# Layer 0 attention: the causal mask is added by VectorE on the way out of PSUM, not accumulated by TensorE

## The reference

```python
def _L0_attn_ref(x, Wq, Wk, Wv, Wo):            # x is the adapter's output for the item
    q, k, v = heads(x @ Wq.T), heads(x @ Wk.T), heads(x @ Wv.T)      # 32 heads of 16
    q = q * cos + rotate_half(q) * sin
    k = k * cos + rotate_half(k) * sin
    scores = jnp.einsum('bhqd,bhkd->bhqk', q, k) / jnp.sqrt(jnp.float32(HEAD_DIM))
    allowed = (j <= i) & (j > i - WINDOW)
    scores = jnp.where(allowed[None, None], scores, -jnp.inf)
    attn = jax.nn.softmax(scores, axis=-1)
    out = jnp.einsum('bhqk,bhkd->bhqd', attn, v)
    return out @ Wo.T
x = x + _L0_attn_ref(_L0_cond_ref(x, L0_cond_weight, itok_B_1_14), L0_attn_Wq, ...)
x = x + _L0_ffn_ref(_L0_cond2_ref(x, ...), ...)
```

## Time and profile before

| | us |
|---|---|
| three runs | 2150.94, 2160.27, 2161.2 |
| their median | 2160.27 |
| the profiled execution's own time | 2157.68 |
| its span in the trace | 2155.9 |

### The profile page before, as it was taken

One profiled execution on the slowest core, in us unless ns is written; L12 is line 12 of the kernel. 1 busy time (PEld: TensorE's weight loads), 2 busy tenths in 40 slices (PEclk: granted clock), 3 DMA queues, 4 the chain that ended last, 5 costly groups with the idle time before them and its releaser, 6 DMA issues.

```text
span 2155.9 us, 35433 instructions
## 1 busy us (share of the span) xinstructions
PE 2037.6 (95%) x12241; PEld 1712.3 (79%) x12264; DVE 1535.5 (71%) x3387; ACT 1334.1 (62%) x3810; POOL 817.1 (38%) x803
## 2 busy tenths in 40 slices
PE   6999977999999999989999999999999999999985
PEld 5777755888888888868888888888888888888863
DVE  5567743566566555558787888888888878888887
ACT  3566652454545445447676777776777767767785
POOL 4100002300000000016666666666566666665774
PEclk9999998999999999989999999999999999999998
DMA  8011101001011100111111121111211111112010
GB/s 291 25 50 45 50 1 69 30 30 64 30 35 64 55 30 21 54 40 49 31 59 50 34 75 31 59 51 33 77 31 60 51 31 60 50 33 78 28 32 30
DMA packets 45009, 108.65 MB, mean 50 GB/s; under 512 B 15634, under 2 KB 21010, under 8 KB 40354
## 3 DMA queue, kind: packets, MB, share of 16 engines
q1 hardware_dynamic: 28450, 72.80, 9.7%
q0 software_dynamic: 16384, 33.59, 5.2%
HBM read 103.20 MB, written 3.15 MB: 49 GB/s over the span
## 4 chain that ended last, share of the span: by engine, by line
PE 84%; DVE 9%; ACT 4%; issue 2%; DMA 0%; POOLq 0%; POOL 0%; SPq 0%; DVEq 0%; ACTq 0%
PE PS L1510 9%; PE PS L1414 8%; PE PS L1276 8%; PE PS L1522 8%; PE PS L1336 7%; PE PS L1477 6%; PE PS L1495 6%; PE PS L1428 4%; PE PS L1289 4%; PE PS L1480 3%; PE PS L344 3%; PE PS L1304 2%; PE PS L1321 2%; PE PS L488 2%; PE PS L334 2%
## 5 line engine op out<-in xcount | busy, mean ns | idle before, releaser
L2345 POOL DMA_INDIRECT kcache<-in_kcache,rows x256 | 253.0, 988 | 563.6 <-DVE x_res L1656 492.9
L1817 DVE CUSTOM_DVE_ANT_0 pr<-PS,ffn_weights,sm 128x640 f32<-128x640 f32 x256 | 225.4, 886 | 128.3 <-PE PS L1480 128.3
L2353 POOL DMA_INDIRECT vcache<-in_vcache,rows x256 | 259.4, 1013 | 137.4 <-PE PS L1304 61.8
L2198 ACT ACTIVATE pr<-pr,sm 128x640 f32<-128x640 f32 x256 | 212.6, 831 | 41.0 <-DVE sm L1817 41.0
L1833 DVE TENSOR_TENSOR prT_lo<-PS,prT_hi 128x512 fp32r<-128x512 f32 x320 | 209.3, 685 | 33.7 <-ACT prT_hi L2209 31.8
L2209 ACT ACTIVATE prT_hi<-PS 128x512 fp32r<-128x512 f32 x320 | 178.8, 596 | 64.7 <-PE PS L1495 56.2
L1495 PE MATMUL PS<-consts,pr 128*128 128x128 f32 x1280 | 174.8, 273 | 9.0 <-issue 5.8
L1495 PEld LDWEIGHTS PS<-consts,pr 128*128 128x128 f32 x1280 | 149.9, 141 | 35.8 <-issue 7.7
L2359 POOL TENSOR_TENSOR vcached_lo<-vcache,vcached_hi 128x512 fp32r<-128x512 f32 x64 | 83.3, 1301 | 250.2 <-ACT vcached_hi L2181 250.2
L2061 ACT ACTIVATE pr<-pr,sm 128x128 f32<-128x128 f32 x256 | 99.8, 391 | 105.7 <-DVE sm L1646 103.7
L1477 PE MATMUL PS<-kT_lo,qT_hi 128*128 128x320 f32 x512 | 154.1, 309 | 0.0
(11 more groups left out here) (322 smaller groups left out, 6354.0 us busy)
## 6 DMA issues: line engine op xcount, KB each, us to landing
arena<-in_wqkv SPq DMA_DIRECT2D x16, 1536.0 KB, 6.3
arena<-in_wo SPq DMA_DIRECT2D x16, 1024.0 KB, 5.3
arena<-in_wcT SPq DMA_DIRECT2D x8, 1024.0 KB, 5.7
kcache<-in_kcache,rows POOLq DMA_INDIRECT x256
vcache<-in_vcache,rows POOLq DMA_INDIRECT x256
arena<-in_xT SPq DMA_DIRECT2D x8, 256.0 KB, 6.4
x_res<-in_x SPq DMA_DIRECT2D x1, 2048.0 KB, 14.5
ffn_weights<-in_alibi SPq DMA_DIRECT2D x2, 1024.0 KB, 6.5
```

Source lines behind the costliest of these rows:

```text
L1817: dve.tensor_tensor_reduce(pr2[:, h, :].rearrange("p (a n) -> p a n", a=2), PS[:, SCORE_BANK[h]:SCORE_BANK[h] + 2, 0:HALF], keymask[:, b, ...
L2198: act.activation(pr2[:, h, :], pr2[:, h, :], ACT.Exp, bias=nm2[:, h:h + 1], scale=-1.0, accum_out=rs2[:, h:h + 1]).then_inc(a2_ex, 1)
L2345: pool.indirect_dma_start(out=kcache[:, c, :], out_offset=None, in_=T["kcache"], in_offset=bass.IndirectOffsetOnAxis(ap=rows[:, g, b, c:c ...
L2353: pool.indirect_dma_start(out=vcache[:, c, :], out_offset=None, in_=T["vcache"], in_offset=bass.IndirectOffsetOnAxis(ap=rows[:, g, b, c:c ...
```

## The change

The mask becomes an fp32 tile `masked` of 128 x 128 (built once, no longer repeated over four heads). The identity products go; the first score products of each bank now start the accumulation. `row_max` adds the mask to a quad's bank with a broadcast over the four heads and writes the sum to the quad's tile of `prob` in SBUF, waits for that result, and reduces it from there; ahead of the add stands a wait that the transposes which last read this tile are done. The exponentials work in place in SBUF. The two waits that guard the score banks are now for the maxima.

```diff
-        causalb = area(17984, GH * P // 2).bitcast(BF16)
+        masked = area(17984, P)
...
-                    pe.wait_ge(s_pr, QUADS * b + 4)
-                for r in range(4):
-                    pe.matmul(bank(r), identb[:], causalb, start=True, stop=True, skip_group_check=True)
+                    pe.wait_ge(s_max, QUADS * b + 4)
                 for t in range(2):
                     for r in range(4):
                         mm = pe.matmul(bank(r, 2 * P, t * 2 * P), qT0[32 * r:32 * r + 32, b % 2, 2 * u + t, :],
                                        kbd[32 * r:32 * r + 32, b % 2, 2 * u + t, :, :].rearrange("p e n -> p (e n)"),
-                                       start=False, stop=True, skip_group_check=True)
+                                       start=(t == 0), stop=True, skip_group_check=True)
...
                 if b + 2 < B:
-                    pe.wait_ge(s_pr, QUADS * (b + 1) + 1)
+                    pe.wait_ge(s_max, QUADS * (b + 1) + 1)
...
             def row_max(b, j):
                 dve.wait_ge(s_sc, 2 * b + j // 4 + 1)
-                dve.tensor_reduce(nmax[:, j % 4, :], heads(bank(j % 4), 4), AX, ALU.min).then_inc(s_max, 1)
+                wait(dve, s_pT, QUADS * b + j - 3)
+                rows = heads(prob[:, j % 4, :], 4)
+                ch.link(dve.tensor_tensor(rows, heads(bank(j % 4), 4), masked.unsqueeze(1).broadcast_to([P, 4, P]),
+                                          ALU.add))
+                dve.tensor_reduce(nmax[:, j % 4, :], rows, AX, ALU.min).then_inc(s_max, 1)
...
-                dve.tensor_scalar(heads(causalb, GH), cst["causal"].unsqueeze(1).broadcast_to([P, GH, P]), -1.0, None,
-                                  ALU.mult).then_inc(s_msk, 1)
+                dve.tensor_scalar(masked, cst["causal"], -1.0, None, ALU.mult).then_inc(s_msk, 1)
...
                 for i in range(4):
-                    op = act.activation(prob[:, j % 4, i * P:(i + 1) * P], bank(j % 4, P, i * P), ACT.Exp,
+                    head = prob[:, j % 4, i * P:(i + 1) * P]
+                    op = act.activation(head, head, ACT.Exp,
                                         bias=nmax[:, j % 4, i:i + 1], scale=-1.0,
                                         accum_out=rsum[:, j % 4, i:i + 1])
```

## The result

The changed kernel takes 2172.57 us (median of 6 runs, 2169.18 to 2176.33), the kernel before beside it 2156.77 (6 runs). The ratio is 1.0073, 95% interval 1.0057 to 1.0089: **15.8 us slower**, more than the 0.5% that can be told from no change. The forecast was 2177 (range 2166 to 2192), with a chance of 0.79 that it is slower. The profiled execution took 2175.28 us (span 2173.5); that of before 2157.68 (span 2155.9).

What follows compares the result with a forecast made beforehand. TensorE was taken to bound the steady cycles (busy 32.29 of 32.50 us). 12.9 + 2.6 + 2.4 = +17.9 us gave 2175.6 on the profiled 2157.68 and 2178.2 on the median 2160.27; forecast 2177, range 2166 to 2192.

Steps and rivals of the forecast that it cites:

- late in the first, second half: Steady cycle: TensorE late by 1.23 us at the residual's transposes and 1.73 at the next y product.
- The removed masks: TensorE's score calls: 0.81 us saved per call where TensorE is the limit; the second call's masks bring nothing.
- The waits: TensorE, every steady cycle: about 0.7 and 0.4 us for normalise 0 and 1, 0.2 residual sum, 1.0 z_gated, 1.3 normalise 4.
- The pair: VectorE's add and reduce per bank: 1.33 us as in layer 1, four taking 5.32 instead of 2.44.
- Cycles 1 to 6: Layer 0's steady cycles: 1.23 + 1.73 - 0.81 = +2.15 us each, six giving 12.9.
- Cycle 0: Layer 0's first cycle: +1.0 us in the first half, +2.45 less 0.81 in the second, +2.6 given.
- Cycle 7: Layer 0's last cycle, a VectorE and ScalarE chain: +2.9 and 0.3 of earlier delays, less 0.81: +2.4 us.
- (a): Rival: VectorE's idle time covers the pair, at 1.0 us or below; 2154 us, thresholds 1.02 and 1.01; chance 0.06.
- (b): Rival: the pair is cheaper than layer 1's, say 1.14 us; 0.63 a cycle, some 2164 us; chance 0.10.
- (c): Rival: TensorE's idle gaps lower its granted clock; +8 us, 2185, or +16 if twice a cycle; chance 0.12.
- (d): Rival: the banks' earlier release removes an unseen limit, so all 16 masks come in; -13 us, 2147; chance 0.02.
- The sum: Whole kernel: 12.9 for cycles 1 to 6, 2.6 for cycle 0, 2.4 for the last, together +17.9 us.

Runs made afterwards that it cites:

- the run without masks: Kernel before with the identity products taken out and nothing in their place, so layer 0 has no causal mask: 2148.22 us, ratio 0.9948.
- the last kernel above: Kernel before with VectorE adding the mask in first halves of cycles 1 to 6, VectorE and ScalarE queues reordered: 2155.3 us, ratio 0.9986.
- the one with cycles 1 to 6 alone: VectorE adds the mask only in cycles 1 to 6; cycles 0 and 7 as in the kernel before: 2172.04 us, ratio 1.0066.
- cycles 0 to 6: Changed kernel with the last cycle (7) undone, its masks on TensorE as before: 2172.39 us, ratio 1.0068.
- edges: VectorE adds the mask only in cycles 0 and 7; cycles 1 to 6 as in the kernel before: 2162.01 us, ratio 1.0017.
- The repeat: The changed kernel measured and profiled once more, nothing altered: 2172.16 us, ratio 1.007 to the kernel before.
- the shorter reduce: Changed kernel with each reduce over the first 64 keys of a head instead of 128: 2157.28 us, ratio 0.9995 to the kernel before.
- one more reduce: Changed kernel with an additional 128x512 reduce in each pair, into scratch nobody reads: 2229.74 us, ratio 1.0326 to the kernel before.
- pair and masks together: Changed kernel with the identity products kept, so the mask is added twice: 2179.9 us, ratio 1.0098 to the kernel before.
- the second half alone: VectorE adds the mask in the second half of each cycle only, TensorE keeps it in the first: 2167.28 us, ratio 1.0039.

## Why the prediction was right, point by point

The time (2172.6 measured, 2177 forecast, inside the range) and the mechanism were right. Of the 4.4 us between the two, 2.1 are the sum (17.9 forecast, 15.8 measured) and 2.3 the time that it was put on (2159.1; the kernel before had a median of 2156.77). Step by step, offsets in us from the first score product, in the second half from the router's:

| step | forecast | measured |
|---|---|---|
| pair of add and reduce | 1.33 | 1.32 |
| maxima start, first half | 1.22 | 1.38 |
| transposes 0 | 7.48 | 7.60 |
| transposes of the residual | 8.91 | 9.01 |
| router scores | 16.92 | 17.02 |
| transposes of z_gated | 4.06 | 4.06 |
| transposes 4 | 10.46 | 10.41 |
| next y product | 11.97 | 11.91 |
| late in the first, second half | 1.23, 1.73 | 1.33, 1.67 |
| masks of the first call | 0.81 | 0.97 |
| steady cycle | +2.15 | +2.04 (cycles 3, 5) |

**The removed masks** are the term that was mis-sized. The chain's 0.81 was the duration of three recorded products; start to start it is 1.98 us from the weighted sums to the scores before (175.50 to 177.48) and 1.01 now (179.87 to 180.88), so 0.97, above even the bound of 0.90. The second call's brought nothing in the whole change and in the run without masks, as forecast (a wait of 0.87 for z_gated; 1.0 was forecast, and the masks there are 0.87). The removal had an effect that the walk left out. VectorE's low part of o doesn't depend on the scores, so with the masks gone the scores move ahead of it and the maxima start 1.38 after them instead of 1.22. With four pairs of 1.32 instead of 1.33 that makes 1.33 late instead of 1.23.

**The waits** were forecast at about 0.7, 0.4, 0.2 (residual sum) and 1.3 us; measured are 0.69, 0.16, none and 1.05. The starts are right all the same: the idle times in brackets count from the modelled ends of products that overlap.

**The pair** is layer 1's, as the earlier trace rows had it. At the reduce the rule of the Trainium skill (VectorE: DVE Perf Modes, "The TRN2 errata") would make the pair 1.27; measured is 1.32, with a pitch of 0.60 for the reduce from SBUF against 0.61 from the bank. Here the measurement speaks against the rule on VectorE. On ScalarE the exponentials from SBUF start 0.39 to 0.40 apart, where four from the bank take 1.37, 0.34 each; the same section gives an SBUF source 52 ScalarE cycles more than a PSUM source, 43 ns by its clock, and that agrees.

```profile
149.13 0.40 ACT L879 ACTIVATE arena<-arena 128x128 f32<-128x128 f32 x1 [2.08 <-DVE arena L642]
...
149.53 0.39 ACT L879 ACTIVATE arena<-arena 128x128 f32<-128x128 f32 x1
```

They stayed beside the path, as forecast.

**Cycles 1 to 6:** 12.9 forecast, 12.0 and 11.1 in the two profiles, 13.7 for these cycles alone by the runs.

**Cycle 0:** +2.6 forecast, 1.0 of it in the first half. Before transposes 4 TensorE waits 5.29 us where it waited 2.41, 2.88 more: that is the 4 x 0.71 by which four pairs are longer than four reduces, of which the forecast let 2.45 in.

```profile
69.42 1.97 PE L407 MATMUL PS<-consts,arena 128*128 128x128 f32 x8 [5.29 <-DVE arena L648]
```

The cycle came out at -0.6 in one profile of the changed kernel and +0.8 in the other, against one profile of before, which the forecast took as exact. More profiles show cycle 0. Where TensorE keeps its masks it took 43.57 (before), 41.19 and 40.86 us (the last kernel above, and the one with cycles 1 to 6 alone); where VectorE adds them 42.96, 44.37, 44.49 and 44.07 (changed, twice, cycles 0 to 6, edges). The first halves, from score to score product, are 27.67 to 29.75 in the former and 27.67 to 28.54 in the latter, so the 1.0 of the first half isn't seen. The second halves are 11.88 to 13.82 and 15.29 to 16.70: they don't overlap, so that part is real. On the mean the cycle is 2.1 longer, with a scatter as large as that; whether it is the 2.6 of the forecast stays open.

**Cycle 7:** +2.4 forecast. That counts the 0.81 of the masks ahead of its scores; from the scores on, as the table counts, it is +3.2. The repeat's +3.3 is that; the first profile's +6.6 has 3.3 more, with a lowered clock. The two waits at its end, 3.96 and 2.70 us:

```profile
310.55 1.45 PE L473 MATMUL PS<-ffn_weights,arena 128*128 128x512 f32 x2 [3.96 <-DVE arena L672]
...
314.71 1.11 PE L478 MATMUL PS<-consts,arena 128*128 128x128 f32 x4 [2.70 <-DVE arena L686]
```

The edges together were forecast at 5.0 and measured alone at 3.6 (1.9 to 5.6 by the interval).

**The rivals.** (a) that idle time covers the pair: refuted by the trace. Of its two thresholds the shorter reduce bears out the first, but for the later start of the maxima, and corrects the second: by the y product it is 0.90 and not 1.01, so that at a pair of 1.0 the second half would still be 0.4 late. (b) a cheaper pair: no, 1.32. (c) the clock: not in the steady cycles of the change, but real one step further (one more reduce); the Trainium skill (TensorE: Matmul & The Clock Gate, "HAM oscillation") describes it, and that run agrees with its transposes at 1.97 us behind a wait of 3.08. The one gap that the rival started from, cycle 0's of 2.41 us, was followed by the lower clock in one profile and by the full one in another. (d) a limit of the banks: no. The run without masks gave one call of two, and pair and masks together, which has the earlier release, is longer by what its two halves are late (1.18 + 1.69), so the release adds nothing.

**The sum** was 17.9. With 2.04 instead of 2.15 for cycles 1 to 6 it would be 17.2, and 14.6 without the 2.6 of cycle 0; measured were 15.8 and 13.6. Over these intervals (3 us) the runs can't tell the two apart.

## What to carry to other kernels

An engine that is 28% idle can still be late: what counts is its queue between one result and the next product that wants it, so compare the end of that queue with the start of that product, and work out the threshold at which it becomes late, for every product behind that queue: here it was the y product that was late first. From the cycles at 1.05 and 1.32 (32.42 and 34.56 us against 32.52) the change would have been even in a steady cycle at a pair of about 1.06, an estimate. Work that TensorE does in 0.97 us is badly moved to an engine that needs 2.9 us for it in such a stretch; only where the moved work is put behind what TensorE wants first, on every queue that it passes (ScalarE's as well), does part of the gain come in. Price removed work from start to start of its neighbours, not by the durations of its rows.

## What the runs showed of the hardware

- The changed kernel's cycles 1 to 5 repeat to 0.01 us in its two profiles, while the time of one program scatters by 7 to 14 us (changed kernel 2167.5 to 2175.5, the second half alone 2159.7 to 2173.8). The scatter goes with the mean granted clock: 0.983 at 2159.7 and 0.976 to 0.977 at 2173.8. It comes from the start, cycles 0, 6 and 7 and the layers behind.
- Waits of up to 1.05 us, five to a cycle of 34.6 us, left the granted clock at 1.00; with waits of 3.1 to 3.4 us it was 0.84 to 0.92. After one wait of 2.41 us it was 0.50 in one profile and 1.00 in another. The extra reduces lengthened the waits and lowered TensorE's busy share together, and no run separates the two.
- A 128x512 reduce on VectorE costs the same from SBUF (0.60 us pitch) as from PSUM (0.61); half of it (128x256) takes 0.34, so the fixed part is some 0.08 us, an estimate (2 x 0.34 - 0.60).
- An add and the reduce that reads it start 0.71 us apart, 0.11 more than two independent ones.
